# Layer 2 of a four-layer kernel: the second block's gate products and the second half's binary products as three products of rounded parts

## The chip, the cores and the metric

One core of a Trainium2 chip runs the whole kernel. The metric is the device time of one execution in microseconds, the median of several runs.

## The reference, cut to what matters

The kernel computes four transformer layers over 1024 tokens of 256 features, each an attention or recurrence part and a feed-forward part. The change lies in layer 2, which is, cut down:

```
xn = layernorm(x)                              # 1024 x 256
i, f, g = silu(xn @ Wi), sigmoid(xn @ Wf), silu(xn @ Wg)
h = scan(h * f + i * (1 - f))                  # over the tokens
x += (rmsnorm(h) * g_norm_weight * g) @ Wo
x += xn @ binarize(weight).T + bias            # the binary feed-forward part, from the same xn
```

Everything is float32. Layer 3 begins with a layernorm of the x that layer 2 leaves and a projection by W_in.

## The kernel before, in words

The order of the work on each engine is written out by hand; the engines meet only at semaphores. `P` is 128 partitions, `BW` 512 tokens (a block, `NB` = 2 of them), `TPB` 4 tiles of 128 tokens in a block, `KD` = 2 halves of the 256 features, `ALL` is `slice(None)`. PSUM is handed out in eight banks of 512 columns (`group`, `reuse`), each given back by the engine that read it.

A float32 value can be multiplied in two ways. `wide` (L602) and `tall` (L611) give float32 operands to TensorE. `split_product` (L621 to L623) takes each operand as two parts, a rounded one ("hi", type float32r) and the rest ("lo"), and adds three products: hi x hi, hi x lo, lo x hi. The rounded part is a copy by ScalarE; the rest is a subtraction, for weights on GpSimd (`rest`, L2218) and for values in PSUM on VectorE. Layers 0, 1 and 3 use parts in most of their products.

Layer 2 goes as follows. The last head of layer 1 ends with VectorE adding gathered rows (L1836, `add_rows`) and the head's output (L1792) to x, and taking statistics (L1577). `normalise` (L1579 to L1590) turns them into xn2 block by block: VectorE writes the variance (L1586), GpSimd raises it to the power -1/2 (L2196, `inverse_deviation`; "the pow" below), and VectorE then subtracts and scales with four tensor_scalar operations (L1590). Behind the first block's xn2 VectorE goes on with the rows of the second block of tokens.

TensorE turns the ternary weights (L1015) and the binary ones (L1032), spends a short stretch on products that keep it busy (L585), turns xn2 into xT (L595), and multiplies: for each block, three gates times two halves (`gate2`, all by `wide`). The transposes of the second block stand before the last gate product of the first. Then come a sum of squares (`mean_square2`, L1040), the binary part for tokens 0 to 511 (`project_ffn2`, by `tall`), the output part for them (`project_z2`), more ternary transposes, the binary part for tokens 512 to 1023, the second sum of squares, and the output part, with the transposes of xn3's first block between. Layer 3's first product is `project_in(0)` at L621 to L623.

ScalarE copies PSUM to xT (`keep_xT`, L1210), copies the ternary weights (L1448, L1450), the turned binary weights (L1456), and computes the sigmoids (L1462, L1463) and silus (L1470). In block 0 the copies of the second block's xT stand before the last silu.

VectorE has, after the second L1590, `recurrence(0)` and `recurrence(1)` (L1979 a product, L1980 the scan, L1982 a square, for each half, then L1985 twice), the variance of the sum of squares (L1990), and then the additions to x: `add_ffn2` (L1594), `add_z2` (L2007 and statistics L1577), `normalise(3, 0)`, `rest_of_xT3(0)` (L2015, the subtraction for the parts of xT3), which `project_in(0)` waits for.

GpSimd fetches rows for layer 1 (L2289), then has the two pows for xn2, then adds the bias to the whole of x (L2336, 2048 columns, when both halves of xn2 are written), the sums of squares' halves (L2341), the rest of W_in's parts (L2218 on lD) and the remaining pows (L2346, L2196). The queue of SyncE isn't touched.

## Time and profile before

| what | us |
|---|---|
| median of 3 runs | 682.6 (681.51 to 683.88) |
| the profiled execution's own time | 687.0 |
| its span | 685.4 |
| TensorE matmuls busy | 638.5 (93%) |
| VectorE busy | 530.8 (77%) |
| ScalarE busy | 344.6 (50%) |
| GpSimd busy | 339.0 (49%) |
| chain that ended last, by engine | PE 56%, DVE 17%, issue 11%, ACT 9% |

A busy share is an average over stages with different limits, so it doesn't tell what one stage is worth. In the profile PE is TensorE, DVE VectorE, ACT ScalarE, POOL GpSimd. The granted clock of TensorE was 1.00 in every stretch read between 535 and 620 us. Layer 2 lies between 546 and 593 us.

### The profile page before, as it was taken

How to read it: one execution, taken by the hardware profiler on the slowest of the kernel's cores; microseconds unless marked ns; L12 is line 12 of the kernel's file. 1: busy time of each engine (PE TensorE's matmuls, PEld its weight loads, DVE VectorE, ACT ScalarE, POOL GpSimd, SP SyncE). 2: the span in 40 equal slices, each digit the busy share in tenths (PEclk: the TensorE clock that was granted, in tenths of full speed). 3: DMA queues.
4: the chain of work that ended last, by engine and by line, in shares of the span. 5: the costliest groups of instructions: out<-in, count | busy, mean ns of one | idle time of the engine just before them, and what ended most of it. 6: DMA issues, size and time to landing. Idle time of an engine off the chain costs nothing.

```text
span 685.4 us, 13485 instructions
## 1 busy us (share of the span) xinstructions
PE 638.5 (93%) x4836; PEld 501.6 (73%) x4836; DVE 530.8 (77%) x1076; ACT 344.6 (50%) x750; POOL 339.0 (49%) x270
## 2 busy tenths in 40 slices
PE   3998999999899999999999999989998899889987
PEld 1455778788478988888898788877977646647766
DVE  4278866698699898988899998575457789779994
ACT  1497222300556475655648565465454473379441
POOL 1054555592367667473867736988328533210000
PEclk9999999999999999999999999999999999999999
DMA  8801000000601001010100101101421200100001
GB/s 249 347 1 56 8 2 1 1 1 0 238 16 40 25 8 38 15 38 23 38 23 8 38 16 56 46 19 44 148 70 39 70 0 1 39 0 1 1 1 62
DMA packets 14647, 31.37 MB, mean 46 GB/s; under 512 B 1837, under 2 KB 8587, under 8 KB 14029
## 3 DMA queue, kind: packets, MB, share of 16 engines
q1 hardware_dynamic: 12813, 26.46, 11.7%
q0 software_dynamic: 1536, 3.15, 1.7%
q10 hardware_dynamic: 256, 1.18, 0.6%
q8 instruction: 28, 0.46, 0.3%
q14 instruction: 14, 0.11, 0.1%
HBM read 26.59 MB, written 5.24 MB: 46 GB/s over the span
## 4 chain that ended last, share of the span: by engine, by line
PE 56%; DVE 17%; issue 11%; ACT 9%; POOL 3%; DMA 3%; another core or an unknown queue 1%; DVEq 0%; SPq 0%; POOLq 0%; ACTq 0%
PE bank L621 10%; PE bank L622 8%; PE bank L623 8%; PE bank L611 7%; PE bank L602 6%; PE bank L814 3%; DVE arena L1767 2%; DVE arena L1766 2%; PE bank L844 2%; PE bank L843 2%; PE bank L828 2%; DVE x L1792 2%; DMA arena<-in_lA 2%; DVE arena L1776 2%; PE bank L717 1%
## 5 line engine op out<-in xcount | busy, mean ns | idle before, releaser
L621 PE MATMUL bank<-zone 128*128 128x256 f32 (+1 forms) x472 | 167.5, 355 | 16.6 <-DVE arena L1767 4.7
L623 PE MATMUL bank<-zone 128*128 128x256 f32 (+1 forms) x472 | 156.5, 331 | 0.0
L622 PE MATMUL bank<-zone 128*128 128x256 f32 (+1 forms) x472 | 156.4, 331 | 0.0
L621 PEld LDWEIGHTS bank<-zone 128*128 128x128 f32 x472 | 88.8, 188 | 42.0 <-issue 15.1
L2256 POOL TENSOR_TENSOR arena<-arena 128x512 f32<-128x512 f32 x64 | 82.1, 1283 | 61.3 <-ACT arena L1343 61.2
L2261 POOL TENSOR_TENSOR arena<-arena 128x512 f32<-128x512 f32 x64 | 83.2, 1300 | 25.3 <-DVE arena L1767 14.0
L623 PEld LDWEIGHTS bank<-zone 128*128 128x128 f32 x472 | 89.0, 188 | 9.1
L622 PEld LDWEIGHTS bank<-zone 128*128 128x128 f32 x472 | 89.3, 189 | 5.3
L1362 ACT ACTIVATE arena<-arena 128x256 f32<-128x256 f32 (+1 forms) x128 | 62.1, 487 | 33.6 <-DVE arena L1776 29.0
L1776 DVE CUSTOM_DVE_ANT_0 arena<-bank,const 128x256 f32<-128x256 f32 (+1 forms) x128 | 45.7, 404 | 29.3 <-PE bank L814 20.7
L1792 DVE SCALAR_TENSOR_TENSOR x<-bank,arena,x 128x256 f32<-128x256 f32 x128 | 53.0, 473 | 9.1 <-PE bank L623 8.4
L1766 DVE TENSOR_TENSOR arena<-bank,arena 64x512 f32<-64x512 f32 x64 | 44.3, 693 | 16.0 <-ACT arena L1343 13.5
L1343 ACT ACTIVATE arena<-bank 128x512 f32<-128x512 f32 x64 | 37.4, 585 | 30.1 <-PE bank L623 30.1
L2218 POOL TENSOR_TENSOR zone<-arena,zone 128x512 fp32r<-128x512 f32 (+1 forms) x42 | 44.5, 1069 | 14.0 <-ACT zone L1427 5.4
L844 PE MATMUL bank<-arena 128*128 128x128 f32 x256 | 49.5, 275 | 1.2 <-issue 1.2
L843 PE MATMUL bank<-arena 128*128 128x128 f32 x224 | 44.9, 282 | 0.1
L1767 DVE TENSOR_TENSOR arena<-bank,arena 64x512 f32<-64x512 f32 x64 | 43.7, 684 | 0.8
L1324 ACT ACTIVATE arena<-bank 128x512 f32<-128x512 f32 x32 | 19.1, 598 | 48.0 <-PE bank L623 48.0
L844 PEld LDWEIGHTS bank<-arena 128*128 128x128 f32 x256 | 40.0, 191 | 3.3 <-issue 2.0
L814 PE MATMUL bank<-arena 128*32 128x160 f32 x896 | 40.9, 307 | 0.0
L2363 POOL TENSOR_TENSOR arena<-arena,minus_half 128x4 f32<-128x4 f32 x2 | 2.0, 1012 | 75.4 <-DVE arena L2066 75.4
L1081 PE MATMUL bank<-zone 128*128 128x512 f32 x128 | 34.4, 407 | 4.4 <-DVE plain L2048 2.2
(296 smaller groups left out, 1329.5 us busy)
## 6 DMA issues: line engine op xcount, KB each, us to landing
arena<-in_qk SPq DMA_DIRECT2D x16, 256.0 KB
arena<-in_tern SPq DMA_DIRECT2D x1, 3072.0 KB, 22.7
arena<-in_wv SPq DMA_DIRECT2D x8, 256.0 KB, 2.8
arena<-in_wo SPq DMA_DIRECT2D x16, 128.0 KB, 2.1
arena<-in_wr SPq DMA_DIRECT2D x1, 1792.0 KB, 10.2
lB<-in_lB SPq DMA_DIRECT2D x1, 1288.5 KB, 25.2
x<-in_x SPq DMA_DIRECT2D x2, 512.0 KB, 8.3
xg_rows<-arena SPq DMA_DIRECT2D x1, 1024.0 KB
```

Source lines behind the costliest of these rows:

```text
L621: pe.matmul(dst, lhi, rhi, start=(n == 0), stop=False)
L622: pe.matmul(dst, lhi, rlo, start=False, stop=False)
L623: last = pe.matmul(dst, llo, rhi, start=False, stop=(n == len(terms) - 1 and not open_end))
L814: last = pe.matmul(ps[2 + g % 2][rows_out, at:at + P + 32], qT1[:, t * P + 32 * i:t * P + 32 * i + 32], kT1[:, t * P - P + 32 * i:t * P + ...
L843: pe.matmul(ps[6 + g // 2][:, tok(t % TPB)], v1[:, t - 1, mine], pT1[:, t, 0, :], start=True, stop=False)
L844: last = pe.matmul(ps[6 + g // 2][:, tok(t % TPB)], v1[:, t, mine], pT1[:, t, 1, :], start=(t == 0), stop=True)
L1362: last = act.activation(S1[:, t, lo:], S1[:, t, lo:], ACT.Exp, scale=-1.0, bias=nmax[:, t:t + 1], accum_out=rsum[:, t:t + 1])
L1766: dve.tensor_tensor(qsin[0:64, j, :], ps[j % 2][64:128, :], sinT[64:128, at], ALU.mult)
L1776: last = dve.tensor_tensor_reduce(S1[:, t, lo:], ps[2 + g % 2][:, tt * 2 * P + lo:(tt + 1) * 2 * P], winmask[:, lo:], -SC1, 3.0e38, ALU.ad ...
L1792: last = dve.scalar_tensor_tensor(out=x[:, t, :], in0=ps[bank][:, tt * D:(tt + 1) * D], scalar=rinv[:, t:t + 1], in1=x[:, t, :], op0=ALU.m ...
L2256: pool.tensor_tensor(qraw[:, j, :], qraw[:, j, :], cosT[:, at], ALU.mult).then_inc(cos_done, 1)
L2261: pool.tensor_tensor((kT1, qT1)[j % 2][:, at], qraw[:, j, :], qsin[:, j, :], ALU.add).then_inc(qk_ready, 1)
```

## The change

For the second block of tokens (512 to 1023) the six gate products, and for the second half of the tokens the binary products, are made of three products of parts. The first block stays in float32.

- The three gate weights get parts, `wg2`: the rounded part by one ScalarE copy of 1536 columns at the end of layer 1, the rest by three GpSimd subtractions of 512 columns, one before the first pow of layer 2 and two between the first and the second. TensorE waits for them before the second block.
- The turned binary weights get parts, `bwT2`: the rounded part by one more ScalarE copy, the rest by one GpSimd subtraction between the second pow and the bias addition.
- The second block's xT isn't copied as float32 any more. ScalarE writes its rounded part to `xT3[0]`, VectorE subtracts the rest into `xT3[1]`, twice 512 columns, ahead of `recurrence(0)`.

```diff
@@ -224,6 +224,7 @@
         held, x_rest, lA_rest = sem("held"), sem("x_rest"), sem("lA_rest")
         x0_hi, x0_split, gu0_hi, gu0_split = sem("x0_hi"), sem("x0_split"), sem("gu0_hi"), sem("gu0_split")
         osq_summed = sem("osq_summed")
+        wg2_hi, wg2_split, x2_hi, bwT_hi, bwT_split = sem("wg2_hi"), sem("wg2_split"), sem("x2_hi"), sem("bwT_hi"), sem("bwT_split")
         qk_full, v_full, wv_hi, wv_split = sem("qk_full"), sem("v_full"), sem("wv_hi"), sem("wv_split")
         win3_hi, win3_split, hid3_hi, hid3_split, hid3_used = (
             sem("win3_hi"), sem("win3_split"), sem("hid3_hi"), sem("hid3_split"), sem("hid3_used"))
@@ -385,6 +386,8 @@
         pr_T = z.grid(NI, D)
         xT3 = [z.grid(KD, T) for _ in range(2)]
         win3 = [z.cols(KD * D) for _ in range(2)]
+        bwT2 = [Carve(zone, z.at + 2 * BW + n * KD * D).grid(KD, D) for n in range(2)]
+        wg2 = [Carve(zone, ZONE - 6 * KD * D - 128 + n * 3 * KD * D).cols(3 * KD * D) for n in range(2)]
         whole3 = Carve(plain, z.at).grid(RING3, BW)
         hid3p = [z.grid(RING3, BW) for _ in range(2)]
         rst3, bias3 = m.cols(T), m.cols(D)
@@ -1021,8 +1024,14 @@
 
             def gate2(n, half, b):
 
-                base = B_W + (1, 0, 2)[n] * KD * D + half * P
-                wide(g_gate2[n][half][b], lambda k: lB[:, base + k * D:base + k * D + P], xT, b)
+                base = (1, 0, 2)[n] * KD * D + half * P
+                if b == 0:
+                    wide(g_gate2[n][half][b], lambda k: lB[:, B_W + base + k * D:B_W + base + k * D + P], xT, b)
+                    return
+                g = g_gate2[n][half][b]
+                reuse(g)
+                split_product(g.ps, [(cut(parts(wg2), ALL, slice(base + k * D, base + k * D + P)), cut(parts(xT3), ALL, k, slice(BW, T)))
+                                     for k in range(KD)]).then_inc(g.full_sem, 1)
 
             pe.wait_ge(bw_ready, 1)
             g = g_bwT
@@ -1041,7 +1050,14 @@
                 last.then_inc(g.full_sem, 1)
 
             def project_ffn2(p):
-                tall(g_ffn2[p], p, lambda t: [(xT[:, k, tok(t)], bwT[:, k, :]) for k in range(KD)])
+                if p < 2:
+                    tall(g_ffn2[p], p, lambda t: [(xT[:, k, tok(t)], bwT[:, k, :]) for k in range(KD)])
+                    return
+                g = g_ffn2[p]
+                reuse(g)
+                for tt in range(2):
+                    last = split_product(g.ps[:, tt * D:(tt + 1) * D], [(cut(parts(xT3), ALL, k, tok(2 * p + tt)), cut(parts(bwT2), ALL, k)) for k in range(KD)])
+                last.then_inc(g.full_sem, 1)
 
             def project_z2(p):
                 pe.wait_ge(z2_ready, KD * (p // 2 + 1))
@@ -1051,6 +1067,8 @@
             turn_xn(2, xn2, 0)
             for b in range(NB):
                 pe.wait_ge(xT_ready, 4 * KD + KD * (b + 1))
+                if b:
+                    pe.wait_ge(wg2_split, 3)
                 for n in range(3):
                     for half in range(KD):
                         if (n, half, b) == (2, KD - 1, 0):
@@ -1063,6 +1081,7 @@
             for p in range(2):
                 project_z2(p)
             turn_ternary(range(4, len(g_wT3)))
+            pe.wait_ge(bwT_split, 1)
             for p in range(2, NT // 2):
                 project_ffn2(p)
             mean_square2(1)
@@ -1449,10 +1468,12 @@
                     else:
                         act.activation(pr_T[:, :, (n - 4) * P:(n - 3) * P].bitcast(F32R), ps16.rearrange("p (q d) -> p q d", q=NI), ACT.Copy).then_inc(g.ready_sem, 1)
 
+            act.activation(wg2[0].bitcast(F32R), lB[:, B_W:B_W + 3 * KD * D], ACT.Copy).then_inc(wg2_hi, 1)
             keep_ternary(range(3))
             keep_xT(2, [0])
             keep_ternary([3])
             act.wait_ge(*g_bwT.full)
+            act.activation(bwT2[0].bitcast(F32R), g_bwT.ps.rearrange("p (k o) -> p k o", k=KD), ACT.Copy).then_inc(bwT_hi, 1)
             act.activation(bwT, g_bwT.ps.rearrange("p (k o) -> p k o", k=KD), ACT.Copy).then_inc(g_bwT.ready_sem, 1)
             for b in range(NB):
                 at = slice(b * BW, (b + 1) * BW)
@@ -1464,7 +1485,9 @@
                 for n in (1, 2):
                     for half in range(KD):
                         if (n, half, b) == (2, KD - 1, 0):
-                            keep_xT(2, [1])
+                            for k in range(KD):
+                                act.wait_ge(*g_xT[2][1][k].full)
+                                act.activation(xT3[0][:, k, BW:T].bitcast(F32R), g_xT[2][1][k].ps, ACT.Copy).then_inc(x2_hi, 1)
                         g = g_gate2[n][half][b]
                         act.wait_ge(*g.full)
                         act.activation((isil, gsil)[n - 1][:, half, at], g.ps, ACT.Silu).then_inc(g.ready_sem, 1)
@@ -1993,6 +2016,9 @@
                 x_is(g_ffn2[p].ready[1] - 1)
                 add_pair(g_ffn2[p], p)
 
+            for k in range(KD):
+                dve.wait_ge(x2_hi, k + 1)
+                dve.tensor_tensor(xT3[1][:, k, BW:T].bitcast(F32R), g_xT[2][1][k].ps, xT3[0][:, k, BW:T], ALU.subtract).then_inc(xT_ready, 1)
             recurrence(0)
             recurrence(1)
             mean_square2(0)
@@ -2329,8 +2355,20 @@
             rest_of_wo(H1 - 1)
             fetch_rows(range(NT + TPB, 2 * NT))
 
-            inverse_deviations(2)
-
+            def rest_of_wg2(n):
+                at = slice(n * KD * D, (n + 1) * KD * D)
+                rest([t[:, at] for t in wg2], lB[:, B_W + n * KD * D:B_W + (n + 1) * KD * D]).then_inc(wg2_split, 1)
+
+            pool.wait_ge(wg2_hi, 1)
+            rest_of_wg2(0)
+            inverse_deviation(2, 0)
+            rest_of_wg2(1)
+            rest_of_wg2(2)
+            inverse_deviation(2, 1)
+
+            pool.wait_ge(bwT_hi, 1)
+            pool.wait_ge(*g_bwT.ready)
+            rest(bwT2, bwT).then_inc(bwT_split, 1)
             pool.wait_ge(xn_ready, 3 * NT)
             pool.wait_ge(bias2_loaded, 16)
             pool.tensor_tensor(x, x, bias2.unsqueeze(1).to_broadcast([P, NT, D]), ALU.add).then_inc(bias2_added, 1)
```

## Rows read from the trace of the kernel before

**Rows 1.** Busy time by stretch: window, length, engines (instructions), granted clock, DMA share, GB/s

```profile
561.40:573.40 12.00, 12.00 (x30) 5.33 (x29) 11.90 (x8) 8.48 (x13) 7.48 (x3) 1.00 0.01 1
```

**Rows 2.** Timeline of TensorE: start, length, line, count, idle time before and its releaser

```profile
544.26 0.28 PE L622 MATMUL bank<-zone 128*128 128x256 f32 x1
...
546.16 0.28 PE L623 MATMUL bank<-zone 128*128 128x256 f32 x1
...
561.41 12.18 PE L602 MATMUL bank<-xT,lB 128*128 128x512 f32 x28
...
574.24 3.70 PE L611 MATMUL bank<-arena,xT 128*128 128x256 f32 x16
...
593.50 0.47 PE L621 MATMUL bank<-zone 128*128 128x512 f32 x1 [2.19 <-issue]
...
603.11 0.40 PE L622 MATMUL bank<-zone 128*128 128x512 f32 x1
...
605.43 0.39 PE L623 MATMUL bank<-zone 128*128 128x512 f32 x1
```

**Rows 3.** Timeline of VectorE

```profile
548.91 1.38 DVE L1590 TENSOR_SCALAR arena<-x,mv,lnw 128x256 f32<-128x256 f32 x4 [1.17 <-POOL lnw L2196]
550.20 0.48 DVE L1836 SCALAR_TENSOR_TENSOR x<-xT,arena,x 128x256 f32<-128x256 f32 x1
...
559.10 1.38 DVE L1590 TENSOR_SCALAR arena<-x,mv,lnw 128x256 f32<-128x256 f32 x4 [1.13 <-POOL lnw L2196]
560.40 0.68 DVE L1979 TENSOR_TENSOR arena<-arena 128x512 f32<-128x512 f32 x1
561.12 5.43 DVE L1980 TENSOR_TENSOR_SCAN arena<-arena 128x512 f32<-128x512 f32 x1
...
567.91 1.22 DVE L1980 TENSOR_TENSOR_SCAN arena<-arena 128x512 f32<-128x512 f32 x1
...
572.12 1.78 DVE L1979 TENSOR_TENSOR arena<-arena 128x512 f32<-128x512 f32 x1
...
587.38 1.38 DVE L1590 TENSOR_SCALAR arena<-x,mv,lnw 128x256 f32<-128x256 f32 x4 [0.53 <-POOL lnw L2196]
...
592.13 1.27 DVE L2015 TENSOR_TENSOR zone<-bank,zone 128x512 fp32r<-128x512 f32 x2
```

**Rows 4.** Timeline of GpSimd

```profile
544.95 1.00 POOL L2289 DMA_INDIRECT arena<-y_rows,arena  x1 [0.31 <-issue]
547.83 1.05 POOL L2196 TENSOR_TENSOR lnw<-lnw,minus_half 128x4 f32<-128x4 f32 x1 [1.88 <-DVE lnw L1586]
...
560.56 4.91 POOL L2336 TENSOR_TENSOR x<-x,bias 128x2048 f32<-128x2048 f32 x1 [1.50 <-DVE arena L1590]
...
571.61 1.74 POOL L2218 TENSOR_TENSOR zone<-lD,zone 128x512 fp32r<-128x512 f32 x1
...
598.18 4.54 POOL L2359 TENSOR_TENSOR x<-x,arena 128x2048 f32<-128x2048 f32 x1 [1.50 <-DVE arena L1590]
```

**Rows 5.** Timeline of ScalarE

```profile
546.93 2.85 ACT L1448 ACTIVATE zone<-bank 128x1024 fp32r<-128x1024 bf16 x3 [3.77 <-PE bank L1015]
...
561.23 1.08 ACT L1210 ACTIVATE xT<-bank 128x512 f32<-128x512 f32 x2
```

**Rows 6.** Timeline of layer 0's parts, VectorE and GpSimd

```profile
55.89 1.39 DVE L1639 TENSOR_SCALAR arena<-arena,const 128x512 f32<-128x512 f32 x1
...
59.28 0.47 DVE L1639 TENSOR_SCALAR arena<-arena,const 128x512 f32<-128x512 f32 x1
...
55.71 2.70 POOL L2218 TENSOR_TENSOR zone<-early,zone 128x512 fp32r<-128x512 f32 x2 [2.55 <-ACT zone L1233]
```

**Rows 7.** Timeline of layer 0's second normalisation, VectorE and GpSimd

```profile
14.83 2.06 DVE L1590 TENSOR_SCALAR arena<-x,mv,lnw 128x256 f32<-128x256 f32 x4 [1.13 <-POOL lnw L2196]
...
14.74 1.04 POOL L2207 MEMSET arena<- 128x544 f32 x2
```

**Rows 8.** Line L1783, layer 1's subtraction from PSUM: durations in ns, min/median/max

```profile
L1783 DVE TENSOR_TENSOR zone<-bank,zone x32: 639/680/692, 214.5 to 543.3; 128x512 fp32r<-128x512 f32 x32
```

## The prediction, made before the changed kernel was run

> **What bounds the kernel now.** I read the shares of the engines by stretch first, then the timelines of TensorE, VectorE, GpSimd and ScalarE from 546 us to 600 us, which is layer 2 and the entry of layer 3. In the stretch of the second block's gates TensorE is busy for all of its 12.00 us, but VectorE is busy for 11.90 us of them as well, so a full TensorE does not yet say that it sets the end [rows 1]. What decides is who waits when the stage is over. TensorE has nothing to do for 2.19 us before the first product of layer 3 at 593.50 us [rows 2]. VectorE's L2015 runs from 592.13 to 593.40 us and is the last input of that product [rows 3]. Followed back, VectorE has no wait for TensorE: L1590 (xn3, 587.38) waited for GpSimd's pow, which waited for VectorE's own statistics, and behind those lie add_z2, add_ffn2, and the two recurrences, without a gap, back to L1979 at 560.40; before it come L1590 at 559.10, the additions L1836 from 550.20, and L1590 at 548.91 [rows 3]. So from 548.9 to 593.4 us the VectorE chain sets the end, with two or three hops over GpSimd's pow, and TensorE, which the chain of waits in the profile names for most of it, is only beside it.
>
> In that chain one link is long for a reason that matters here. The scan L1980 at 561.12 takes 5.43 us, and 1.22 us elsewhere [rows 3]. GpSimd's addition of the bias over all of x runs from 560.56 to 565.47 [rows 4]; the scan ends 1.08 us behind it. L1979 at 572.12 takes 1.78 us instead of 0.68 and ends 0.55 us behind GpSimd's L2218 of 571.61 to 573.35 [rows 3, 4]. An operation of VectorE with two SBUF operands stands still while a GpSimd operation runs.
>
> **Part 1, TensorE's products.** An f32 product of one k leaves two records. The 28 of L602 take 12.18 us, the last of them about 0.6 of it, so one comes every (12.18 - 0.60)/27 = 0.429 us. The second block has 6 products x 2 k x 2 = 24: 10.30 us. As three products of rounded parts there are 36 of 512 columns. Ten intervals lie between 603.11 and 605.43, 0.232 us each: 8.35 us. For the second half's binary products, 16 records take (3.70 - 0.38)/15 = 0.221 us each, 3.54 us for two pairs; in place of them come 24 of 256 columns at (546.16 - 544.26)/16 = 0.119 us, 2.85 us [rows 2]. TensorE saves 1.95 + 0.69 = 2.6 us. All of it lies beside the VectorE chain, so I count it as 0. The idle 2.19 us before layer 3 only grows.
>
> **Part 2, ScalarE.** It gains the 1536 columns of wg2's rounded part and the 512 of bwT2's. A copy of 1024 columns takes about 1.0 us (three in 2.85), so the first costs some 1.6 us; it stands in an idle time of 3.77 us [rows 5]. The second, some 0.6 us, goes ahead of the sigmoids of block 0, whose results VectorE first wants at 560.4: 0. The copies of xT for the second block only change their target. If this cover were gone it would cost 0.6 us.
>
> **Part 3, GpSimd's three parts of wg2.** Each is L2218 with 512 columns, two of which take 2.70 us [rows 6], so at most 1.35. The first starts when the last fetch of rows is over, at 544.95 + 1.00, and ends at about 547.3, before the pow can start at 547.83 [rows 4]. Beside it VectorE adds from PSUM and takes statistics, with one SBUF tensor each. I count 0; if the statistics, which no row shows beside a GpSimd operation, were held too, it would be up to 1.3.
>
> The second and third have no wait ahead of them and stand directly behind the pow, whose end releases VectorE's L1590 as well. L1590 is on the chain. The same pattern is in the trace once: in layer 0 the two memsets of 1.04 us follow the pow at 14.74, GpSimd is first by 0.09 us, and the four L1590 take 2.06 us instead of the 1.38 of 548.91 [rows 3, 7]: 0.68, the block less some 0.36. The other tensor_scalar, L1639, takes 1.39 beside an L2218 and 0.47 alone, 0.92 more, and GpSimd's pair is hardly stretched [rows 6]; for two operands L1979 gives 1.10 more. The bounds for each part are 0 (L1590 not held by this form) and 1.35; I take 1.0, between the 0.92 and 1.10 of the nearest rows. The two parts give +2.0 us, on xn2's first half and on everything behind it. TensorE's first gate product comes later by as much, VectorE's own chain too.
>
> **Part 4, GpSimd's part of bwT2.** It waits for things long ready, so it stands directly behind the next pow, the one that releases the L1590 of 559.10, and meets it [rows 3]. Again 0 to 1.35; I take +1.0. The bias addition waits for that L1590 and so keeps its place behind it.
>
> The Trainium skill (SBUF — State Buffer, "Who interferes with whom") says that GpSimd and a VectorE instruction with two SBUF inputs, or in a two-port mode, exclude each other for a whole instruction; L1979 and L1590 agree in kind, but the memsets cost 0.36 less than their length. By that rule's full length the three parts would give 3 x 1.35 = 4.1 us where I take 3.0.
>
> **Part 5, VectorE's two subtractions.** They are new, 0.64 to 0.69 us each [rows 8], and stand ahead of the recurrence. Let e be the end of the second L1590 (560.48 before). Before, the first scan ended at 566.55 = e + 6.07. Now ScalarE's copies end at about e + 1.8 (561.23 + 1.08 - 560.48) [rows 5] and the subtractions at e + 2.5. They read PSUM and one SBUF tensor, and in 32 instances of that shape, most beside GpSimd's L2256 and L2261, none took over 0.692 us [rows 8], so they pass the bias addition. It begins at e + 0.08 and takes 4.54 us when nothing holds it (598.18) [rows 4]: e + 4.62. L1979 ends 0.55 later, the scan 1.22 + 0.04 later: e + 6.43. So two operations cost only **+0.36** us, since the wait for the bias addition was there already. Bounds: 0, and 1.6 if the subtractions were held as well (the first rival below). TensorE's second block waits for them, too, but a product of block 0 still fills it until about e + 2.6.
>
> TensorE's new waits: wg2_split is complete near 552 and needed near 566, bwT_split near 562 and needed after 580. Behind them nothing queues.
>
> **Sum.** 2.0 + 1.0 + 0.36 = +3.4 us against the profiled execution of 687.0 us (its span is 685.4): 690.4. That execution stands 4.4 us over the median of the runs; applied to the median, 682.6 + 3.4 = **686.0 us**.
>
> **Rivals.** (a) The subtractions are held by the bias addition. They would end at e + 4.62 + 1.25, then L1979 0.68 and the scan 1.26: e + 7.8, 1.4 more than in my sum, +4.8, 687.4 us. For it: the reader waits at just that place. Against: rows 8. Chance 0.07; with a held statistics operation the upper end is about 688.5.
>
> (b) L1590 isn't held by a GpSimd operation that reads. Then only the third part of wg2 counts: it meets the L1836 at 550.20, with two SBUF operands, +1.1, and the sum is 1.1 + 0.36 = +1.5: 684.1 us. Against: L1590 was held for 0.68 and L1639 for 0.92. Chance 0.13. The Trainium skill (VectorE: DVE Perf Modes, "What auto-detection actually checks") has a single-source operation with source and target in SBUF in the two-port mode, so by it this rival falls; the trace's 2.06 us for four L1590 beside the memsets is what bears that out.
>
> (c) TensorE, not VectorE, ends the stage, and the three parts find VectorE idle. Then the time falls by Part 1's 2.6 us less 0.36: 680.4 us, faster. It decides if VectorE's L2015 at 592.13 is released by work that ends with TensorE's; for it, the chain of waits puts TensorE on most of the stretch. Against: the 2.19 us gap, and VectorE's 11.90 of 12.00 us. Chance 0.06.
>
> (d) The parts fall between VectorE's operations and cost nothing: +0.4, 683.0 us. The release by one pow speaks against it. Chance 0.10.
>
> **Numbers.** Forecast 0.64, (a) 0.07, (b) 0.13, (c) 0.06, (d) 0.10. A measurement of this kernel can tell about 0.3%, 2.05 us, from no change: faster is below 680.55, slower above 684.65. (b) and (d) end mostly within it, as does a small part of the forecast's own spread, with the terms near their lower bounds; slower 0.74, same 0.20, faster 0.06. The range leaves out (c) and the lower part of (d): 683.0 to 688.5.
>
> **What would show it.** Right: the four L1590 of xn2 take some 3.4 us for the first half and 2.4 for the second, with L2218 beside them; the scan still takes 4 to 5 us or L1979 takes its place; TensorE's gap before layer 3 is larger than 2.19 us although its own work is 2.6 us less; L2015's distance from the first L1590 grows. Wrong: L1590 at 1.38 us in both halves (then b or d), subtractions of several us (a), or no gap at TensorE before layer 3 (c).

## The result, and the profile of the changed kernel

| | before | after |
|---|---|---|
| median | 682.76 us (20 runs) | 685.52 us (20 runs) |
| ratio, 95% interval | | 1.0040 [1.0027, 1.0054] |
| span of the profiled execution | 685.4 us | 683.7 us |

The changed kernel is slower by 2.8 us, 0.4% of its time, and the interval leaves out no change. The two profiled executions, taken singly, say the opposite, 1.7 us faster. Most of that lies ahead of the change. Between layer 1's eight additions from PSUM (L1792, L1815 after) and the first L1590 of layer 2 (L1613 after), where the change adds only a ScalarE copy and GpSimd's first part, the profile of before has 18.84 us and that of after 16.48. Of the twelve other kernels below, seven of the eight in the first two groups have 16.48 or 16.49 (the eighth moves work into this code), and the four of the last group have 18.82 to 18.90, whatever they changed. It goes with the group of runs and not with what the kernels change; whether the chip makes it, no run here tells.

So I compare a stretch inside each trace: from the start of the first L1590 of layer 2 to the end of the rounded rest of xn3 (L2015, L2041 after), which the first product of layer 3 needs. Before it is 593.40 - 548.91 = 44.49 us [rows 3]. After it is 47.36 us, 2.87 more, and the measured difference is 2.76.

The timeline of VectorE of the kernel after, over this stretch: start, length, line, operation, count, idle time before and its releaser.

```profile
544.39 2.93 DVE L1613 TENSOR_SCALAR arena<-x,mv,lnw 128x256 f32<-128x256 f32 x4 [1.16 <-POOL lnw L2222]
547.25 0.47 DVE L1859 SCALAR_TENSOR_TENSOR x<-xT,arena,x 128x256 f32<-128x256 f32 x1
...
556.12 2.32 DVE L1613 TENSOR_SCALAR arena<-x,mv,lnw 128x256 f32<-128x256 f32 x4 [1.12 <-POOL lnw L2222]
559.49 1.29 DVE L2021 TENSOR_TENSOR zone<-bank,zone 128x512 fp32r<-128x512 f32 x2 [1.05 <-ACT zone L1490]
560.70 2.94 DVE L2002 TENSOR_TENSOR arena<-arena 128x512 f32<-128x512 f32 x1
563.67 1.22 DVE L2003 TENSOR_TENSOR_SCAN arena<-arena 128x512 f32<-128x512 f32 x1
...
590.48 1.27 DVE L2041 TENSOR_TENSOR zone<-bank,zone 128x512 fp32r<-128x512 f32 x2
```

The timeline of GpSimd beside it:

```profile
541.12 1.10 POOL L2244 TENSOR_TENSOR zone<-lB,zone 128x512 fp32r<-128x512 f32 x1
543.31 1.04 POOL L2222 TENSOR_TENSOR lnw<-lnw,minus_half 128x4 f32<-128x4 f32 x1 [1.10 <-DVE lnw L1609]
544.35 2.18 POOL L2244 TENSOR_TENSOR zone<-lB,zone 128x512 fp32r<-128x512 f32 x2
...
556.06 1.26 POOL L2244 TENSOR_TENSOR zone<-arena,zone 128x512 fp32r<-128x512 f32 x1
558.52 4.57 POOL L2374 TENSOR_TENSOR x<-x,bias 128x2048 f32<-128x2048 f32 x1 [1.20 <-DVE arena L1613]
```

Against [rows 3] the three differences can be read off. The first four L1590 take 2.93 us instead of 1.38, with two of GpSimd's parts (L2244) from 0.04 us before them: +1.55. The second four take 2.32 instead of 1.38, with the third part in the same place: +0.94. The end of the second group is e = 558.44; the first scan ends at 564.89 = e + 6.45, where it ended at e + 6.07: +0.38. The sum is 2.87, the whole difference of the stretch. The scan is short now, 1.22 us, and L2002 ahead of it (L1979 before) long, 2.94: it ends 0.55 us behind the bias addition, at 563.64.

The timeline of TensorE of the kernel after: the first and last of the second block's 36 gate products, and the end of layer 2.

```profile
560.84 0.50 PE L624 MATMUL bank<-zone 128*128 128x512 f32 x1
...
569.11 0.40 PE L626 MATMUL bank<-zone 128*128 128x512 f32 x1
...
586.29 1.68 PE L598 MATMUL bank<-const,arena 128*128 128x128 f32 x8 [1.71 <-DVE arena L1613]
587.77 3.58 PE L614 MATMUL bank<-lB,arena 128*128 128x256 f32 x8
591.85 0.47 PE L624 MATMUL bank<-zone 128*128 128x512 f32 x1 [0.50 <-issue]
```

Busy time by stretch of the same kernel: window, length, PE, PEld, VectorE, ScalarE, GpSimd (instructions), granted clock, DMA share, GB/s.

```profile
587.80:591.30 3.50, 3.50 (x10) 2.32 (x8) 2.37 (x6) 0.82 (x2) 1.01 (x1) 0.52 0.00 0
591.80:594.60 2.80, 2.75 (x12) 2.31 (x13) 2.03 (x9) 0.69 (x1) 0.58 (x1) 1.00 0.03 6
```

The 36 products come one every 8.27/35 = 0.236 us and take 8.5 us, against some 10.3 us for the 24 of before at the spacing in [rows 2]. The gain is there and buys nothing: TensorE stands idle for 1.71 us before it may turn xn3. It isn't even seen as a longer gap before layer 3, which is 0.50 us instead of 2.19 [rows 2]. Right behind the idle time the granted clock is 0.52, TensorE's 1.2 GHz level, and the eight last z2 products take 3.58 us instead of the 1.89 that the same eight take at full clock in other kernels below. They fill the gap.

### The profile page after: what moved, and what is told of

It is laid out like the page before. It is cut to its first block, busy times and chain, and to the rows that moved or that the text cites. A ratio compares the mean times of both kernels' runs of the same rounds, so it can differ in the third digit from the quotient of the medians.

```text
span 683.7 us, 13535 instructions
## 1 busy us (share of the span) xinstructions
PE 637.5 (93%) x4856; PEld 504.2 (74%) x4856; DVE 532.3 (78%) x1078; ACT 346.2 (51%) x752; POOL 343.1 (50%) x274
## 3 DMA queue, kind: packets, MB, share of 16 engines
q0 software_dynamic: 1536, 3.15, 1.8%
## 4 chain that ended last, share of the span: by engine, by line
PE 51%; DVE 19%; ACT 11%; issue 10%; DMA 3%; POOL 3%; SPq 0%; DVEq 0%; POOLq 0%; ACTq 0%
PE bank L624 9%; PE bank L626 8%; PE bank L625 8%; PE bank L614 5%; PE bank L605 4%; PE bank L817 3%; PE bank L847 2%; PE bank L831 2%; DVE arena L1790 2%; PE bank L846 2%; DVE arena L1789 2%; DVE x L1815 2%; DMA arena<-in_lA 2%; ACT arena L1381 1%; PE bank L720 1%
## 5 line engine op out<-in xcount | busy, mean ns | idle before, releaser
L624 PE MATMUL bank<-zone 128*128 128x256 f32 (+1 forms) x492 | 174.6, 355 | 13.1 <-DVE arena L1790 3.2
L626 PE MATMUL bank<-zone 128*128 128x256 f32 (+1 forms) x492 | 163.5, 332 | 0.0
L625 PE MATMUL bank<-zone 128*128 128x256 f32 (+1 forms) x492 | 163.3, 332 | 0.0
L624 PEld LDWEIGHTS bank<-zone 128*128 128x128 f32 x492 | 92.7, 189 | 39.5 <-issue 13.9
L626 PEld LDWEIGHTS bank<-zone 128*128 128x128 f32 x492 | 92.7, 188 | 9.7
L625 PEld LDWEIGHTS bank<-zone 128*128 128x128 f32 x492 | 93.1, 189 | 5.9
L1815 DVE SCALAR_TENSOR_TENSOR x<-bank,arena,x 128x256 f32<-128x256 f32 x128 | 53.0, 474 | 8.8 <-PE bank L626 8.0
L2244 POOL TENSOR_TENSOR zone<-arena,zone 128x512 fp32r<-128x512 f32 (+1 forms) x43 | 45.7, 1071 | 10.0 <-DMA arena<-in_cossin 4.8
```

The source lines that it names most:

```text
L624: pe.matmul(dst, lhi, rhi, start=(n == 0), stop=False)
L625: pe.matmul(dst, lhi, rlo, start=False, stop=False)
L626: last = pe.matmul(dst, llo, rhi, start=False, stop=(n == len(terms) - 1 and not open_end))
L1815: last = dve.scalar_tensor_tensor(out=x[:, t, :], in0=ps[bank][:, tt * D:(tt + 1) * D], scalar=rinv[:, t:t + 1], in1=x[:, t, :], op0=ALU.m ...
```

## Experiments: the parts of the change one by one

The first four kernels ran on one chip, with 29 runs of the kernel before (median 681.58 us). A difference in us is the ratio less 1, times that median, as everywhere below. The diffs are cut to the lines that carry the step; `...` stands for what is left out.

**TensorE's side alone.** GpSimd's three parts of wg2, its part of bwT2 and VectorE's two subtractions are gone. This leaves out the rounded rests of the weights and of xT: the products take the rounded part in their place, so TensorE issues the same 36 and 24.

```diff
-            rest_of_wg2(0)
-            rest_of_wg2(1)
-            rest_of_wg2(2)
-            rest(bwT2, bwT).then_inc(bwT_split, 1)
...
-            for k in range(KD):
-                dve.wait_ge(x2_hi, k + 1)
-                dve.tensor_tensor(xT3[1][:, k, BW:T].bitcast(F32R), g_xT[2][1][k].ps, xT3[0][:, k, BW:T], ALU.subtract).then_inc(xT_ready, 1)
```

> TensorE's side of the change alone: the products are as many and as long as in the changed kernel, but the rounded part stands in for the rest in both operands, and GpSimd's four subtractions and VectorE's two are left out. If the VectorE chain sets the end of layer 2, the 2.6 us that TensorE saves are worth nothing: 0.0 us against the kernel before, within 0.6, and from the first L1590 of layer 2 to the end of rest_of_xT3(0) it takes the 44.5 us of before. If TensorE sets it (rival c), 2.6 us less than before.

Measured 681.93 us, ratio 0.9996 [0.998, 1.0011]; stretch 44.56 us, +0.07. A gain of 2.6 us is excluded, in the timed runs and in the stretch of the trace: TensorE doesn't set the end of this stage, and rival (c) falls.

**Without GpSimd's parts.** As above, but VectorE's subtractions stay; the rests of the weights are left out.

```diff
-            rest_of_wg2(0)
-            rest_of_wg2(1)
-            rest_of_wg2(2)
-            rest(bwT2, bwT).then_inc(bwT_split, 1)
```

> The changed kernel without GpSimd's four subtractions for the weights; the rounded part of the weights stands in for the rest. VectorE's two subtractions stay. If the whole cost but the 0.38 us of the delayed scan comes from GpSimd holding VectorE's L1590, this takes 0.4 us more than the kernel before (2.5 less than the changed one), and all eight tensor_scalar operations of xn2 take 1.38 us a four. If the two subtractions cost their own 1.3 us, 1.3 more than before.

Measured 681.88 us, ratio 1.0001 [0.9987, 1.0016]; stretch 44.90 us, +0.41, both groups of L1613 at 1.38 us, scan end at e + 6.46. The subtractions cost what the trace had them cost, and the time is back at that of before. ScalarE's two added copies are still made here, so they aren't what cost the rest.

**GpSimd's parts alone.** All products stay float32 as before and VectorE's subtractions are gone; only the parts are made.

```diff
-                if b == 0:
-                    wide(g_gate2[n][half][b], lambda k: lB[:, B_W + base + k * D:B_W + base + k * D + P], xT, b)
-                    return
...
+                wide(g_gate2[n][half][b], lambda k: lB[:, B_W + base + k * D:B_W + base + k * D + P], xT, b)
...
-                if p < 2:
+                if True:
...
-            for k in range(KD):
-                dve.wait_ge(x2_hi, k + 1)
-                dve.tensor_tensor(xT3[1][:, k, BW:T].bitcast(F32R), g_xT[2][1][k].ps, xT3[0][:, k, BW:T], ALU.subtract).then_inc(xT_ready, 1)
```

> The kernel before with the parts of the weights made and not used: ScalarE's two copies and GpSimd's four subtractions are added, TensorE, the copies of xT and VectorE stay as before. If GpSimd's subtractions hold VectorE, this is 2.5 us slower than the kernel before (1.55 at the first L1590, 0.94 at the second), with TensorE doing exactly the old work. If the cost came with TensorE's or VectorE's new work, 0.

Measured 684.51 us, ratio 1.0044 [1.0029, 1.006]: +3.0 us, the whole loss with no change of precision anywhere in the products. Its timeline of VectorE, and the first twenty gate products on TensorE with the busy time beside them:

```profile
543.28 2.93 DVE L1605 TENSOR_SCALAR arena<-x,mv,lnw 128x256 f32<-128x256 f32 x4 [1.16 <-POOL lnw L2211]
...
555.01 2.32 DVE L1605 TENSOR_SCALAR arena<-x,mv,lnw 128x256 f32<-128x256 f32 x4 [1.13 <-POOL lnw L2211]
557.60 4.88 DVE L1994 TENSOR_TENSOR arena<-arena 128x512 f32<-128x512 f32 x1 [0.27 <-ACT arena L1485]
562.51 1.22 DVE L1995 TENSOR_TENSOR_SCAN arena<-arena 128x512 f32<-128x512 f32 x1
...
547.77 11.91 PE L605 MATMUL bank<-xT,lB 128*128 128x512 f32 x20 [0.74 <-ACT xT L1223]
...
548.00:553.00 5.00, 5.00 (x6) 1.96 (x7) 4.79 (x13) 3.98 (x6) 0.00 (x0) 0.50 0.01 2
```

Both groups are as long as in the kernel after, to the hundredth. The scan ends at e + 6.40 although there is no subtraction: ScalarE's silu (L1485) is late here, L1994 waits 0.27 us for it, the bias addition has begun in the meantime and holds L1994 for 4.88 us. The silu is late since TensorE's granted clock was 0.50 in this stretch of this execution: the twenty products take 11.91 us, where they take 8.85 at 1.00 in the kernel after. So of this kernel's +2.81 us the two collisions make 2.49, and the other 0.3 go back to the clock in this one execution. When L1979 gets in first, as in [rows 3], the bias addition doesn't hold it at all and its 0.68 us are hidden beside the addition. In the kernel after it is the subtractions that put L2002 behind the start of the bias addition, and its +0.38 is this and no sum of their own 1.3 us.

**Two parts earlier.** ScalarE's copy of wg2 is made in the last head of layer 1, and GpSimd's first two parts stand ahead of the second set of row fetches. Nothing is left out.

```diff
+            pool.wait_ge(wg2_hi, 1)
+            rest_of_wg2(0)
+            rest_of_wg2(1)
             rest_of_wo(H1 - 1)
             fetch_rows(range(NT + TPB, 2 * NT))
-            pool.wait_ge(wg2_hi, 1)
-            rest_of_wg2(0)
+            rest_of_wg2(2)
             inverse_deviation(2, 0)
-            rest_of_wg2(1)
-            rest_of_wg2(2)
             inverse_deviation(2, 1)
```

> The changed kernel with the weights' parts moved: ScalarE's copy goes into its idle time in the last head of layer 1, two of GpSimd's three subtractions into GpSimd's idle time there, the third to the place ahead of the first pow. Nothing is behind that pow any more. The first L1590 should return to 1.38 us and the kernel be 1.55 us faster than the changed one, 1.3 slower than before (0.94 of bwT2 and 0.38 stay). If the two moved subtractions hold the additions L1836 of the last head on VectorE's chain instead, up to 1 us of it is lost again. If a rival cause (ScalarE's copies, the new waits) made the cost, nothing changes.

Measured 685.97 us, ratio 1.0058 [1.004, 1.0076], +4.0 us where 1.3 was expected. The stretch did what was expected (45.83 us, +1.34, the first group at 1.39 us). The loss had moved ahead of it. The timelines of GpSimd, VectorE and TensorE of this kernel ahead of layer 2:

```profile
534.55 2.13 POOL L2246 TENSOR_TENSOR zone<-lB,zone 128x512 fp32r<-128x512 f32 x2
...
533.82 3.16 DVE L1861 SCALAR_TENSOR_TENSOR x<-xT,arena,x 128x256 f32<-128x256 f32 x1
537.01 0.83 DVE L1861 SCALAR_TENSOR_TENSOR x<-arena,x 128x256 f32<-128x256 f32 x1
...
541.91 0.58 PE L624 MATMUL bank<-zone 128*128 128x256 f32 x1 [1.39 <-DVE zone L1808]
```

Busy time of the same kernel in the last products of layer 1:

```profile
541.90:544.60 2.70, 2.69 (x12) 2.69 (x13) 2.40 (x7) 0.00 (x0) 2.09 (x2) 0.50 0.41 93
```

Two parts of wg2 and the part of wo behind them hold two operations of VectorE (L1861, L1836 before, 0.48 us each when alone) for 3.0 us. By the trace the first of them had started 0.73 us ahead of the parts; why it is held even so, no run here tells. TensorE waits 1.23 and 1.39 us for L1808, and in the next stretch the granted clock is 0.50, so the last products of layer 1 run at half speed. The stretch from the eight additions to layer 2 is 18.86 us where its neighbours on this chip have 16.48. What the same GpSimd work costs depends on what stands beside it on VectorE, and a place where GpSimd itself is idle isn't a free place.

## Experiments: a version that avoids the collisions

The next four kernels ran on one chip too, with 35 runs of the kernel before (median 681.46 us). Nothing is left out of the computation in them.

**Parts by the clock of VectorE.** Parts two and three of wg2 wait until VectorE's additions of layer 1 (L1859) are through, so that they run beside additions from PSUM and statistics; the part of bwT2 goes ahead of the second pow.

```diff
             rest_of_wg2(0)
             inverse_deviation(2, 0)
+            pool.wait_ge(combined, 12)
             rest_of_wg2(1)
+            pool.wait_ge(combined, 16)
             rest_of_wg2(2)
+            pool.wait_ge(bwT_hi, 1)
+            pool.wait_ge(*g_bwT.ready)
+            rest(bwT2, bwT).then_inc(bwT_split, 1)
             inverse_deviation(2, 1)
-            pool.wait_ge(bwT_hi, 1)
-            pool.wait_ge(*g_bwT.ready)
-            rest(bwT2, bwT).then_inc(bwT_split, 1)
```

> The changed kernel with GpSimd's parts moved into the stretches in which VectorE has statistics and additions from PSUM: the second part of wg2 waits until the gathered rows of tiles 4 and 5 are added, the third and bwT2's until those of tiles 6 and 7 are. The amount of work is the changed kernel's. If a GpSimd operation costs VectorE only when it meets an operation with two SBUF operands or a tensor_scalar, both L1590 return to 1.38 us and the whole is 0.4 to 0.7 us slower than the kernel before, 2.1 to 2.4 faster than the changed one; the second pow may start up to 0.3 us late. If any VectorE operation is held, the cost moves to the statistics and the time stays at the changed kernel's.

Measured 683.12 us, ratio 1.0018 [0.9998, 1.0038]; stretch 44.99 us, +0.50. Its timelines of GpSimd and VectorE:

```profile
545.63 1.09 POOL L2244 TENSOR_TENSOR zone<-lB,zone 128x512 fp32r<-128x512 f32 x1 [3.33 <-DVE x L1859]
549.15 1.09 POOL L2244 TENSOR_TENSOR zone<-lB,zone 128x512 fp32r<-128x512 f32 x1 [2.43 <-DVE x L1859]
550.19 1.27 POOL L2244 TENSOR_TENSOR zone<-arena,zone 128x512 fp32r<-128x512 f32 x1
...
542.34 1.38 DVE L1613 TENSOR_SCALAR arena<-x,mv,lnw 128x256 f32<-128x256 f32 x4 [1.16 <-POOL lnw L2222]
...
545.58 0.88 DVE L1815 SCALAR_TENSOR_TENSOR x<-bank,arena,x 128x256 f32<-128x256 f32 x2
546.50 0.75 DVE L1600 BATCH_NORM_STATS2 stats<-x 128x6 f32<-128x256 f32 x2
...
552.61 1.38 DVE L1613 TENSOR_SCALAR arena<-x,mv,lnw 128x256 f32<-128x256 f32 x4 [1.13 <-POOL lnw L2222]
```

The same three parts, now beside L1815 (one operand in PSUM) and the statistics, cost next to nothing: these take 0.88 and 0.75 us as they do alone, both groups of L1613 take 1.38, and only the short L1609 takes 0.27 us instead of 0.17. So 2.37 of the stretch's 2.87 us were a matter of place. In the timed runs this kernel is at +1.2 us [-0.1, 2.6], so there the gain is known only roughly.

**The bias on TensorE.** GpSimd's addition of the bias over all of x is gone. The bias, times 1/64, is put in rounded part (64 partitions) and rest (64 partitions), and one product with ones for each tile adds it in PSUM. First in the kernel before, then in the kernel after:

```diff
-            pool.wait_ge(bias2_loaded, 16)
-            pool.tensor_tensor(x, x, bias2.unsqueeze(1).to_broadcast([P, NT, D]), ALU.add).then_inc(bias2_added, 1)
...
+            act.activation(ones2.bitcast(F32R), ones, ACT.Copy)
+            act.activation(bp.bitcast(F32R), bias2, ACT.Copy, scale=1.0 / 64).then_inc(bias_hi, 1)
...
+            dve.scalar_tensor_tensor(out=bp[64:128, :].bitcast(F32R), in0=bias2[64:128, :], scalar=1.0 / 64, in1=bp[64:128, :],
+                                     op0=ALU.mult, op1=ALU.subtract).then_inc(bias2_added, 1)
...
+                    last = pe.matmul(g.ps[:, tt * D:(tt + 1) * D], ones2.bitcast(F32R), bp.bitcast(F32R), start=False, stop=True)
```

> The kernel before with GpSimd's 4.5 us addition of the bias over all of x taken away: TensorE adds the bias inside the binary products instead, as one more product of rounded parts for each tile (8 of 256 columns, 0.95 us in all); VectorE makes the rest of the bias after recurrence(0) (0.4 us), ScalarE two small copies. The first scan is no longer held, so VectorE's chain is shorter by 4.15 - 0.4 = 3.7 us. TensorE, in float32 for both blocks and 0.95 us longer, then becomes what is late: of its 2.19 us of idle time before layer 3 only 1.2 are left, so the kernel should gain about 1.2 us, not 3.7, and TensorE's gap before layer 3 should be gone. If TensorE were no limit, 3.7.

In the kernel before: 679.57 us, ratio 0.9978 [0.9958, 0.9997], -1.5 us; stretch 43.44 us, -1.05. The scan takes 1.22 us, 4.2 less, but most of that is lost again, to a wait that hadn't been there. Two rows of VectorE's timeline:

```profile
572.81 0.87 DVE L2020 SCALAR_TENSOR_TENSOR x<-bank,arena,x 128x256 f32<-128x256 f32 x2 [1.07 <-PE bank L612]
...
582.03 0.88 DVE L2020 SCALAR_TENSOR_TENSOR x<-bank,arena,x 128x256 f32<-128x256 f32 x2 [1.77 <-PE bank L612]
```

VectorE now waits for TensorE, four times, 0.34 + 1.07 + 0.60 + 1.77 = 3.8 us: with its long link shortened the bound has moved, and of TensorE's gap before layer 3 0.49 us are left. So the float32 products had been close to setting the end.

> The changed kernel with the same removal of GpSimd's bias addition; the rest of the bias is made on VectorE while it waits for ScalarE's copies. The two subtractions of the second block are no longer hidden behind the bias addition, so VectorE gains only about 2.2 us, not 4: from the end of the second L1590 the first scan ends after 4.2 us instead of 6.45. The whole is 0.6 us slower than the kernel before. If the subtractions had cost nothing by themselves, 4.1 less than the changed kernel.

In the kernel after: 682.97 us, ratio 1.0017 [0.9998, 1.0036]; stretch 45.12 us, +0.63, that is 2.24 us less than the kernel after. The first scan ends at e + 4.19 instead of e + 6.45; the two collisions with the L1613 stay.

**Both together**, with the subtractions put between the first recurrence's product and its scan, where they fill a wait:

```diff
                     chain(dve.tensor_tensor(isil[:, half, at], isil[:, half, at], fneg[:, half, at], ALU.mult))
+                    if b == half == 0:
...
+                        for k in range(KD):
+                            dve.wait_ge(x2_hi, k + 1)
+                            dve.tensor_tensor(xT3[1][:, k, BW:T].bitcast(F32R), g_xT[2][1][k].ps, xT3[0][:, k, BW:T], ALU.subtract).then_inc(xT_ready, 1)
```

> Both together, and VectorE's first L1979 ahead of the rest of the bias and the two subtractions: the parts are in the free stretches, the bias is on TensorE, and TensorE has the 2.6 us that the change saves. VectorE's chain is then shorter than that of the kernel before by 6.07 - 3.65 = 2.4 us and TensorE's by 1.7 with 2.2 us of idle time to use. Expected 2.4 us faster than the kernel before, within 0.7; if TensorE's saving were of no use in any arrangement, no better than bias_on_pe.

Measured 678.5 us, ratio 0.996 [0.9942, 0.9979]: 2.7 us faster than the kernel before and, taken over two groups of runs, some 5.5 faster than the changed one. The stretch is 42.23 us, -2.26. Here the shorter products are worth something: it is 1.21 us shorter than with the bias on TensorE alone, because VectorE's waits for TensorE are gone; one of 1.12 us, for GpSimd's L2397, is back, which the kernel before has as well.

## Experiments: the granted clock behind TensorE's idle time

In four profiles the fall of the clock hit the twelve products that open layer 3, which everything in layer 3 waits for. The timeline of TensorE of the kernel with its side alone (the first and last of the twelve, then the next line), and the busy time of the kernel with timed parts:

```profile
587.10 0.47 PE L624 MATMUL bank<-zone 128*128 128x512 f32 x1 [2.19 <-issue]
...
591.28 0.39 PE L626 MATMUL bank<-zone 128*128 128x512 f32 x1
591.51 0.86 PE L1100 MATMUL bank<-zone 128*128 128x512 f32 x3
```

```profile
585.00:587.40 2.40, 0.24 (x2) 0.00 (x0) 2.37 (x6) 0.00 (x0) 0.00 (x0) 1.00 0.00 0
587.40:589.00 1.60, 1.57 (x6) 1.34 (x7) 1.53 (x5) 0.00 (x0) 0.00 (x0) 0.88 0.04 10
589.00:591.60 2.60, 2.60 (x7) 2.02 (x7) 1.44 (x8) 0.69 (x1) 1.01 (x1) 0.50 0.00 0
```

From 587.10 to 591.51 is 4.41 us, where the kernels before and after have 2.83 and 2.84. Three of the four have two gaps of TensorE, 1.7 us before xn3 is turned and 2.19 us before layer 3; the fourth, with the bias on TensorE, has the second alone. So has the kernel before, and its clock stays at 1.00: the gap alone doesn't tell it. From the end of the rounded rest to the end of the span it is 93.55 to 93.60 us in these four, and 91.92 to 92.00 in before, after and the four others of the two groups.

Were it so in every execution, and never in the kernel before, each of the four would be 1.6 us slower than its stretch says. The table says otherwise.

| kernel | stretch, us | behind it, us | sum | measured, us |
|---|---|---|---|---|
| TensorE's side alone | +0.07 | +1.60 | +1.7 | -0.3 [-1.4, 0.7] |
| without GpSimd's parts | +0.41 | +1.55 | +2.0 | +0.1 [-0.9, 1.1] |
| parts timed | +0.50 | +1.57 | +2.1 | +1.2 [-0.1, 2.6] |
| bias on TensorE, after | +0.63 | +1.59 | +2.2 | +1.2 [-0.1, 2.5] |
| the kernel after | +2.87 | -0.05 | +2.8 | +2.8 [1.8, 3.7] |
| GpSimd's parts alone | +2.81 | -0.08 | +2.7 | +3.0 [2.0, 4.1] |
| bias on TensorE, before | -1.05 | -0.08 | -1.1 | -1.5 [-2.9, -0.2] |
| timed parts and bias | -2.26 | -0.02 | -2.3 | -2.7 [-4.0, -1.4] |
| two parts earlier | +1.34, and +2.38 ahead | -0.02 | +3.7 | +4.0 [2.7, 5.2] |

The last five agree within 0.4 us. The first four lie 0.9 to 2.0 us under their sum, and within 0.7 of the stretch alone.

The fall is no matter of one kernel or one place. TensorE has a gap of 2.11 to 2.17 us in layer 1 too, at some 460 us, in code that no kernel here changes, and behind it the clock fell in eight of the fourteen profiles and stayed in six. Before and after, the first product behind the gap and the busy time soon after:

```profile
462.65 0.50 PE L621 MATMUL bank<-zone 128*128 128x512 f32 x1 [2.12 <-POOL zone L2218]
...
463.60:466.60 3.00, 3.00 (x21) 1.63 (x20) 0.00 (x0) 0.60 (x1) 2.23 (x4) 0.50 0.35 98
```

```profile
462.22 0.50 PE L624 MATMUL bank<-zone 128*128 128x512 f32 x1 [2.16 <-POOL zone L2244]
...
463.20:466.20 3.00, 3.00 (x28) 2.02 (x28) 1.39 (x5) 1.21 (x4) 2.24 (x4) 1.00 0.32 96
```

So one profile can't say what a kernel's clock does in its other executions. Their record can in part, since it has each one's mean granted clock. It differs between executions of one kernel, and the time with it: of the 35 of the kernel before in the second group, the thirteen at 0.999 took 680.2 us on average and the sixteen at 0.994 took 682.3. The kernel before has a mean of 0.9959, 0.9963 and 0.9950 in the three groups, less than the 0.997 of its own profile, so it loses time to falls that its profile doesn't show. The first four of the table are only 0.0004 to 0.0015 lower than it, where one fall as in their profiles is about 0.0025 (1.7 of 681 us, summed from the clock in stretches of 2 us). Part of the 1.6 us is then likely in the kernel before as well. This explanation fits the first four rows, but it rests on means, which don't tell where a fall was, so it isn't shown.

It also bears on the main result, since the clock fell inside the stretch in the profile of GpSimd's parts alone. Of that kernel's twelve executions the four at 1.000 took 682.95 us on average, and the four of the kernel before at 0.999, in the same group, 679.79: the loss is there, 3.2 us, where the clock hardly fell.

I filled the gaps, in four kernels on a third chip (29 runs of the kernel before, median 686.96 us):

```diff
+            stay_busy(g_xT[3][0][0], D, 6)
             turn_xn(3, xn3, 0)
...
+            stay_busy(g_xh3[0][0], D, 8)
             pe.wait_ge(win3_split, 1)
             project_in(0)
```

> tensor_alone (leaves out both rounded rests, as there) with the same useless products in the two gaps. In tensor_alone's trace the twelve products of project_in(0) take 4.41 us instead of 2.83 after gaps of 1.73 and 2.19 us, and from their start to the end of the span it is 93.5 us instead of 91.9, yet its measured time was that of the kernel before. Theory A (the fall happens in the timed runs too, and eats a gain of about 1.6 us that the shorter products bring elsewhere): project_in(0) back at 2.83, 1.6 us faster than tensor_alone, ratio 0.9975 against the kernel before. Theory B (the fall is a matter of the profiled execution alone): same time as tensor_alone, ratio 1.000.

Measured 687.46 us, ratio 1.0001 [0.9983, 1.002] (the rests are left out here as in the kernel that it builds on).

> parts_timed with the same useless products in the two gaps. Its stretch is +0.50 us, its project_in(0) takes 4.26 us instead of 2.83, and it measured +1.2 us against the kernel before. Theory A (the clock's fall costs the rest of the measured loss): project_in(0) 2.83, start of it to span end 91.9 us, time +0.5 or less, ratio 0.9985 to 1.0007. Theory B (the fall does not happen in the timed runs): +1.2 us again, ratio 1.0018. If neither: the fillers delay the transposes or project_in(0) themselves, visible as a gap of 0.0 before them and a later start.

Measured 688.39 us, ratio 1.0000 [0.9981, 1.0018].

> Kernel after with useless products on TensorE in its two gaps ahead of layer 3: six of 128x256 before the transposes of xn3's first half (1.71 us idle after) and eight between the last z2 products and project_in(0) (0.50 us idle after). In the kernel after the clock granted falls to 0.52 at 587.80 and the last eight z2 products take 3.58 us instead of 1.89, but end 0.4 us before the rounded rest of xT3 does (591.75). Theory (the fall of the clock costs nothing here, since VectorE's chain sets when layer 3 starts): z2 back at 1.89 us, stretch to project_in(0) unchanged at 47.4 us, time 0.0 against the kernel after, so +2.8 us against the kernel before, ratio 1.004. Rival (the fall of the clock is part of the measured 2.8): up to 1.7 us less, ratio 1.0015 to 1.002.

Measured 691.53 us, ratio 1.0051 [1.0031, 1.0071].

> timed_and_bias with five useless products of 128x256 in its one remaining gap (1.60 us before project_in(0)). Its project_in(0) already takes 2.82 us at full clock, so a control: same time as timed_and_bias (3.0 us under the kernel before, ratio 0.996) by both theories; slower by 0.2 us or more only if the fillers run past the end of the rounded rest.

Measured 684.32 us, ratio 0.9952 [0.9932, 0.9972] (five fillers in its one gap). The timeline of TensorE with timed parts and fillers:

```profile
585.55 2.75 PE L588 MATMUL bank<-const 128*128 128x256 f32 x12
588.14 1.04 PE L598 MATMUL bank<-const,arena 128*128 128x128 f32 x8
589.01 1.89 PE L614 MATMUL bank<-lB,arena 128*128 128x256 f32 x8
590.74 3.62 PE L588 MATMUL bank<-const 128*128 128x256 f32 x16
594.01 0.59 PE L624 MATMUL bank<-zone 128*128 128x512 f32 x1
```

The clock held at this place, project_in(0) is back at some 2.9 us (594.01 to 596.95 here), but I had sized the fillers wrongly. Each leaves two records, eight take 3.6 us in a gap of 2.19, and the first product of layer 3 starts 1.11 us behind the rounded rest (592.90) where it was 0.10 before. The part behind the stretch is 93.1 us: of the 1.6 us to be recovered 0.5 were. In the kernel after, where the gap was 0.50, it starts 2.51 us behind, and its profile has the clock at 0.50 in block 0's gate products besides, as in GpSimd's parts alone; so its +3.5 us is no clean repeat of the +2.8. The times alone decide nothing here.

The executions' clocks say more. With fillers the mean is 0.9970 in the first two kernels, 0.0020 above the kernel before of this group; without them, on other chips, it had been 0.0006 and 0.0015 below it. By an estimate from these numbers the fillers gave back 0.0026 and 0.0035 of some 685 us, 1.8 and 2.4 us of full clock. So the fall isn't a matter of the profiled execution alone (theory B), which is one of the timed ones anyway. What theory A says it costs, 1.6 us in every execution, isn't shown either: a gain and the fillers' own overrun can't be told apart in these times. The losses and gains go the same way on this chip, at +3.5 us for the kernel after and -3.3 for both together. Timed parts are at 0.0 within 1.3 us, where they had been at +1.2.

## Why the prediction was right, and where it was not

The forecast was +3.4 us and slower; +2.8 was measured, and the mechanism is the one forecast. By its steps:

- **What bounds the kernel**: right. TensorE's products alone gave nothing, so the VectorE chain sets the end. What carried the reading was that VectorE has no wait for TensorE anywhere in the stretch, not the busy shares. The bound was near, though: 3.8 us of waits for TensorE came up when the scan was freed.
- **Part 1**, 2.6 us of TensorE's time at 0: right, -0.3 [-1.4, 0.7] measured. Rival (c) is out.
- **Part 3**, first part of wg2 at 0: right, it ran beside an addition from PSUM and the statistics, which kept 0.75 us. The open question there, whether statistics are held, is answered by this and by the timed parts: no.
- **Part 3**, second and third part at +2.0: right in kind, too large, 1.55. This is the mis-sized term, by 0.45 us. Its length was off: a part that reads lB takes 1.09 us, not the 1.35 of layer 0's pair [rows 6], and the loss of the nearest held operations (0.92, 1.10) was taken over from those longer ones. The loss lies under GpSimd's length each time, by 2.18 - 1.55 = 0.63 for the pair, 1.26 - 0.94 = 0.32 for the single one and 1.04 - 0.68 = 0.36 for the pair of memsets of [rows 7]. Two parts cost twice 0.32, but the memsets don't, so a fixed amount for each instruction isn't shown.
- **Part 4** at +1.0: 0.94.
- **Part 5** at +0.36: 0.38 in the kernel after, 0.41 without the other parts; the two subtractions take 1.29 us beside the bias addition, some 0.64 each, so rival (a) is out. It comes from the wait that was there already, as forecast: with the bias addition gone, the same subtractions and their wait for ScalarE are no longer free (scan end e + 4.19 against e + 1.86). Rivals (b) and (d) fall with the 2.93 and 2.32 us.
- **The Trainium skill**: SBUF — State Buffer, "Who interferes with whom", has the two engines shut out each other for a whole instruction. The three parts last 2.18 + 1.26 = 3.44 us and cost 2.49. So the kind of operation that is held agrees, also in what is not held (an operand in PSUM), and the price by full length is 0.95 us too high here.
- **The sum**: 1.55 + 0.94 + 0.38 = 2.87 in the trace, 2.76 measured.
- **What would show it**: the four L1590 at 2.93 (some 3.4 forecast) and 2.32 (2.4), and L1979 in place of the scan were right. One sign was wrong. "TensorE's gap before layer 3 is larger than 2.19 us": it is 0.50. By the prediction's own list, a gap that is gone would point to rival (c), and this one is most of the way there. The step that failed there is the overlap: the saved time went into a gap of 1.71 us ahead of xn3's turning and not into the old one, and a slower clock stretched the eight products behind it by 1.7 us into the old gap. A gap tells of slack only when the clock beside it is read too.

## What to carry to other kernels

A GpSimd operation that is free by the shares of busy time isn't free beside a VectorE operation on the chain with both inputs, or its only input and its output, in SBUF. It cost 0.65 to 0.75 of its length where both were released together, and nearly all of it beside layer 1's additions (3.0 of 3.05 us with two parts earlier). It cost nothing beside one with an input in PSUM or beside statistics, nor beside L1979 in [rows 3], which had started 0.16 us ahead of the bias addition; starting first wasn't enough for L1861. Work put directly behind an instruction that releases VectorE starts together with what it releases: place it by waiting for the step after. Before making a busy engine faster, look for who waits for it; and when a long link of the bounding chain is cut, price again, since the other engine may be the bound by then.

## What the runs showed of the hardware that I had not expected

- The same GpSimd subtraction, 128x512 with the same types, takes 1.08 to 1.13 us with its source in lB and 1.26 to 1.27 with its source in arena, in each of the kernels above that have it. Why, no run here tells.
- The granted clock fell from 1.00 to 0.50 to 0.52 behind gaps of TensorE of 1.4 to 2.2 us near layer 3 or ahead of layer 2 in six profiles, in two behind three gaps of 0.7 us one after the other, and not behind the gap of 2.19 us in the kernel before. Behind one and the same gap of 2.1 to 2.2 us in layer 1 it fell in eight of fourteen. A faster product can so make the products behind it slower, in some executions and not in others.
- A wait of 2.4 us in layer 1 came and went with the group of runs, in kernels that don't differ there. It is nearly as large as the loss studied, so single spans were of no use and only the stretch beside the change was.
